# The maxima of full attention reach their rows by a transfer of two-byte elements, where a 32x32 transposition on VectorE stood

## The reference, cut to what matters

```
h = layernorm(x)
q, k, v = h @ Wq, h @ Wk, h @ Wv                 # 16 heads of 8
s = einsum('bhtd,bhsd->bhts', q, k) / sqrt(8)    # 1024 x 1024 for each batch and head
m = max(s, axis=-1)                              # one maximum for each query
e = exp(s - m)
out = (e @ v) / sum(e) @ Wo (+ bo)
x = x + out
```

## Time and profile before

| what | value |
|---|---|
| median of 3 runs | 1250.81 us (1248.14 to 1253.72) |
| the profiled execution's own time | 1252.19 us |
| its span in the profile | 1250.5 us |
| full attention, first layer, first to last splitting by POOL | 446.2 to 750.5 us |
| full attention, second layer | 874.2 to 1177.3 us |
| DVE busy over the whole span | 897.3 us, 72% |

### The profile page before, as it was taken

One profiled execution on the slowest core, in us unless ns is written; L12 is line 12 of the kernel. 1 busy time (PEld: TensorE's weight loads), 2 busy tenths in 40 slices (PEclk: granted clock), 3 DMA queues, 4 the chain that ended last, 5 costly groups with the idle time before them and its releaser, 6 DMA issues.

```text
span 1250.5 us, 32345 instructions
## 1 busy us (share of the span) xinstructions
PE 1065.1 (85%) x12934; PEld 532.7 (43%) x12934; DVE 897.3 (72%) x1221; ACT 741.3 (59%) x1496; POOL 184.7 (15%) x341
## 2 busy tenths in 40 slices
PE   6457887888648799999999998877999999999986
PEld 3135676764214333333334444533333344444443
DVE  4554554556465479999999991364899999999635
ACT  2250222223822339989999994222599899999921
POOL 9500434330008000000000000000000000000000
PEclk9668878779977799999999998678999999999977
DMA  2140212100000523322010100007322300101000
GB/s 82 64 126 23 85 56 85 52 2 1 1 0 0 174 83 67 70 48 49 18 29 18 26 21 20 0 1 227 59 62 52 77 20 20 26 20 27 19 14 34
DMA packets 65913, 58.05 MB, mean 46 GB/s; under 512 B 24944, under 2 KB 50032, under 8 KB 65648
## 3 DMA queue, kind: packets, MB, share of 16 engines
q1 hardware_dynamic: 65776, 56.14, 17.1%
HBM read 29.08 MB, written 26.84 MB: 45 GB/s over the span
## 4 chain that ended last, share of the span: by engine, by line
DVE 39%; PE 27%; issue 17%; POOL 8%; DMA 4%; ACT 3%; SPq 2%; POOLq 0%; DVEq 0%; ACTq 0%
DVE nmf L1355 33%; PE wide L565 16%; PE bank L565 10%; POOL big L535 4%; DMA KQs<-m_dram 3%; ACT xcsq L931 2%; DVE xcsq L1138 1%; DVE nmt L1364 1%; DVE res L1138 1%; SPq L371 1%; ACT big L931 1%; POOL KQs L502 1%; DVE big L1439 1%; DVE x L1138 1%; DMA kq_dram<-big 1%
## 5 line engine op out<-in xcount | busy, mean ns | idle before, releaser
L1355 DVE TENSOR_REDUCE nmf<-wide 128x1 f32<-128x1024 f32 x512 | 586.9, 1201 | 34.7 <-PE wide L565 34.5
L931 ACT ACTIVATE big<-wide 128x512 f32<-128x512 f32 (+2 forms) x773 | 441.9, 601 | 149.3 <-PE wide L565 116.1
L565 PE MATMUL bank<-big,V 128*9 128x128 f32 x8192 | 319.2, 274 | 11.8
L565 PE MATMUL wide<-big,KQs 48*128 48x512 bf16 x1024 | 308.0, 381 | 4.3 <-DVE nmf L1355 3.2
L931 ACT ACTIVATE big<-bank 128x512 f32<-128x512 f32 (+3 forms) x489 | 237.5, 506 | 82.4 <-PE bank L689 61.5
L565 PEld LDWEIGHTS bank<-big,V 128*9 128x9 f32 x8192 | 176.7, 90 | 232.2 <-ACT big L931 222.0
L565 PE MATMUL wide<-KQs,big 50*128 50x512 bf16 x683 | 233.5, 381 | 8.0 <-DMA KQs<-m_dram 6.9
L565 PE MATMUL bank<-KQs,big 50*128 50x512 bf16 x341 | 130.0, 381 | 4.2 <-DMA KQs<-m_dram 3.2
L547 POOL CAST nms<-nmf 128x4 bf16<-128x4 f32 x128 | 23.8, 186 | 715.5 <-DVE nmf L1355 715.5
L1302 DVE TENSOR_REDUCE nm<-wide 95x11 f32<-95x1408 f32 x32 | 51.7, 1620 | 57.5 <-PE wide L565 57.4
L565 PEld LDWEIGHTS wide<-KQs,big 50*128 50x128 bf16 x683 | 52.4, 93 | 83.4 <-ACT big L931 56.0
(11 more groups left out here) (190 smaller groups left out, 1050.6 us busy)
## 6 DMA issues: line engine op xcount, KB each, us to landing
kq_dram<-big SPq DMA_DIRECT2D x48, 256.0 KB, 4.1
o_dram<-big SPq DMA_DIRECT2D x128, 64.0 KB, 1.6
KQs<-k_dram SPq DMA_DIRECT2D x48, 132.0 KB
big<-kq_dram SPq DMA_DIRECT2D x32, 192.0 KB, 4.1
KQs<-kq_dram SPq DMA_DIRECT2D x32, 192.0 KB, 4.6
KQs<-q_dram SPq DMA_DIRECT2D x16, 293.9 KB
m_dram<-nmt SPq DMA_DIRECT2D x128, 8.0 KB
KQs<-m_dram SPq DMA_DIRECT2D x128, 2.0 KB
```

The source lines that it names most:

```text
L565: return nc.tensor.matmul(o, l, r, start=start, stop=stop, **kw)
L931: return nc.scalar.activation(o, i, f, **kw)
L1355: nc.vector.tensor_reduce(nmf[:, (s0 + i) % 4, c:c + 1], wide[:, k:k + 2, :].rearrange("p g c -> p (g c)"), AX.X, ALU.max, negate=True).th ...
```

## The change

DVE's transposition goes, with its semaphore nm_turned. SP now waits for POOL's split itself and sends columns 0 to 7 of nms straight to m_dram, with the two dimensions exchanged in the destination: the element of partition q and column j goes to row j, place q. Neighbours in the source are 256 bytes apart in the destination, so each two-byte element is a piece of its own. m_dram keeps its size; rows 8 to 31, which nobody read, are no longer written. `shift` is as before.

Two waits change with it. POOL may write a buffer of nms again only when the transfer that read it four slots earlier has landed (nm_out). DVE, before piece 0 of a slot, waits until POOL's split four slots earlier is done, because it reuses nmf; the transposition's wait used to cover that.

```
             def turned(i):
                 s = s0 + i
-                sp.wait_ge(nm_turned, s + 1)
-                sp.dma_start(m_dram[i, :, :].rearrange("j (g q) -> g j q", g=4),
-                             nmt[:, s % 4, :]).then_inc(nm_out[s % 4], 16)
+                sp.wait_ge(nm_split, s + 1)
+                sp.dma_start(m_dram[i, 0:8, :].rearrange("j q -> q j"),
+                             nms[:, s % 4, 0:8], allow_slow_non_contiguous=True).then_inc(nm_out[s % 4], 16)
...
         def split_shift(s):
             pool.wait_ge(mx_read, 4 * (s + 1))
             if s >= 4:
-                pool.wait_ge(nm_turned, s - 3)
+                pool.wait_ge(nm_out[s % 4], 16 * (s // 4))
...
             def maximum(i, c):
                 n = 4 * (s0 + i) + c
+                if c == 0 and s0 + i >= 4:
+                    dve.wait_ge(nm_split, s0 + i - 3)
                 dve.wait_ge(mx_ready, n + 1)
...
-            def turn(i):
-                s = s0 + i
-                dve.wait_ge(nm_split, s + 1)
-                if s >= 4:
-                    dve.wait_ge(nm_out[s % 4], 16 * (s // 4))
-                nc.vector.transpose(nmt[:, s % 4, :], nms[:, s % 4, :]).then_inc(nm_turned, 1)
-
             for i in range(SLOTS):
                 for c in range(4):
                     maximum(i, c)
-                    if c == 0 and i:
-                        turn(i - 1)
                 if i % H == 6 and i > H:
                     reciprocal(layer, i // H - 1)
-            turn(SLOTS - 1)
```

More of the change, by code:

```diff
@@ L195, in build @@
         mx_ready, mx_read = sem("mx_ready"), sem("mx_read")
-        nm_first, nm_split, nm_turned = sem("nm_first"), sem("nm_split"), sem("nm_turned")
+        nm_first, nm_split = sem("nm_first"), sem("nm_split")
         nm_out = [sem(f"nm_out{i}") for i in range(4)]
```

## The result

| | before | after |
|---|---|---|
| median of 4 runs of each, side by side | 1252.26 us | 2591.9 us (2582.0 to 2601.75) |
| ratio, 95% interval | | 2.071 [2.064, 2.079] |
| span of the profiled execution | 1250.5 us | 2599.7 us |
| POOL's first to last split, first layer | 304.3 us | 952.8 us |
| the same, second layer | 303.1 us | 954.9 us |

The forecast was 1302 us. The sign was right, the size was 26 times too small (1340 us more against 50), and the time lies far outside the range. The two attention layers hold 1300 of the 1349 us by which the span grew.

A forecast was written before the change was run, and what follows sets the result against it. DVE was taken to bound the ordinary slot at 4.62 us, the maxima's path almost as tight. With +34 us from 100 ordinary slots and +18 from 24 late ones, 1252.2 became 1304, as median 1302 us; range 1222 to 1410.

The forecast's parts named there:

- DVE sets the ordinary slot: Reductions and transposition on DVE set the slot's 4.62 us; without the transposition, 0.14 us less, 4.49.
- The path: Maxima's way from POOL's split through SP's transfers to PE's scores: a second bound, afterwards 3.50 us plus delay.
- slack of 2.0 us: From issue of the transfer back into qop to the scores, up to 2.0 us costs nothing.
- the saving of 0.72: Between POOL's end and SP's issue, the transposition's going takes 0.72 us a slot off the path.
- The DMA's pace of packets: In SP's queue, 1024 packets at 0.53 per ns take 1.98 us, making the transfer back 1.46 us later.
- rival A: Transfer out hides on 16 engines, 0.69 us for its packets, delay 0.17; kernel faster, 1225 us; chance 0.30.
- The transfer itself lands with a whole slot in hand: Transfer out to m_dram: its landing costs nothing, because `shift` of a slot is issued only a slot later.
- Rival C: Two-byte DRAM writes may cost more than 64-byte ones: 1399 us, or over 1800 at 24.6 ns; above 1400, chance 0.13.
- rate of 12 us for every 0.1 us a slot: Every 0.1 us that the transfer out's 1024 packets take beyond 1.6 us costs the kernel 12 us.
- B's better end: Rival that the change comes out even, 1258 us at worst; at a delay of 1.0, 1248 us; chance 0.09.
- The estimate from "VectorE: DVE Perf Modes": Transfer out's 1024 elements, by a page calling transposing plain DMA 19 times slower: 1.6 us, sum near no change.

The follow-up runs named there:

- e7: Kernel before without DVE's transposition, nms sent in the old 64-byte runs, exchange of partition and row left out: 1235.8 us beside 1251.7.
- e4: Kernel before plus one unread transfer a slot of 1024 two-byte elements into SBUF, each partition writing its own place: 1333.6 us beside 1254.0.
- e6: Kernel before without m_dram and transposition: eight transfers a slot write two-byte neighbours from nms straight into qop's rows in SBUF: 2047.7 us beside 1251.7.
- e1: Kernel before plus, in each slot, the changed kernel's transfer of 1024 two-byte elements to an unread DRAM tensor: 2622.3 us beside 1254.0.
- e5: Kernel before without m_dram and transposition: pieces take every fourth query, two transfers write eight-byte packets straight into qop's rows: 1239.6 us beside 1251.7.

## Why the prediction was wrong

*DVE sets the ordinary slot, and gains by the transposition's going: right, the size some 40% too large (0.13 for 0.09 us a slot).* e7 shows the reductions back to back and 4.53 us for the predicted 4.49.

*The path with its slack of 2.0 us and the saving of 0.72: right where it could be tried.* e4 gives 5.25 for a worked-out 5.23. In the changed kernel both terms are buried.

*The DMA's pace of packets: wrong, to the other side.* I took the common pace of 0.53 packets per ns of the earlier trace rows as a limit, 1.98 us for 1024. Behind an empty queue they pass in about 0.7 us, as rival A had it, 7.3 ns each on 16 engines. The nearness of two paces in rows of other shapes was a coincidence, and what the trace said of engine time per packet (10.8 ns) was the better guide. Quick packets delay the transfer back by 0.34 us (e4), not 1.46. Had this been all, the path would have given 3.50 + 0.34 = 3.84 and DVE's bound would have ruled: a gain of about 1%, as e7 shows it.

*"The transfer itself lands with a whole slot in hand": this is the step that failed.* I put all of the cost into the queue and gave the landing none beyond its packets. It takes 13 to 17 us, three slots' worth. All else follows from it: `shift` waits for it (944.9 us), transfers land one after the other, the next `shift` is held behind the next one, PE gets a slot's scores every 15.1 us, DVE starves, and PE's clock falls. 128 slots of 15.1 - 4.8 = 10.3 us are 1318 of the 1340 us, of which some 125 come from the slots beside the loads, when the DMA engines are busy with few bytes; that term wasn't in the prediction either.

*Rival C had the right sentence and the wrong mechanism and price.* A small write may cost more than the row of 64 bytes tells: true. But I priced it as time on an engine (up to 24.6 ns, a period of 9.3), and in the slots without loads the engines aren't busy (0.08 of the time), while the period is 14.0. Beside the loads, and in e6, they are, so the mechanism of C has a share there. Its rate of 12 us for every 0.1 us a slot was right (128 x 0.1 = 12.8); it was tied to the time of the packets, where it holds for the time to landing.

*B's better end* has a small slip: by the sum of the prediction a delay of 1.0 gives 1251 - 12 + 7 = 1246, not 1248.

The prediction quoted the Trainium skill, "DMA: Bandwidth & Descriptors", Specifications, that transfers under 512 bytes are read, modified and written. The runs bear it out only in part: neither 64 bytes nor two bytes alone in their piece (2.7 us) show a large price, but many small ones in one piece do. Such an update of a piece, one after another, is a reading that fits the table; no row shows the update itself. The estimate from "VectorE: DVE Perf Modes" (1.6 us, 19 times the transposing transfer) is short of the measured 14.6 by a factor of 9. From the first I should have made a rival that is priced by the landing, and given C more than 0.13.

What stays open: why 8 writes in 64 bytes cost 0.8 us and 16 cost 5 to 7, which size the piece has, and where between the last packet and the semaphore the time is spent. That a transfer behind lands late is shown for the one queue of SP, with 2 KB (e1) and with loads of 192 KB behind.

## What to carry over

When a transfer turns columns into rows, look at how many separate elements of it fall next to one another at the destination, not only at their number: the records of packets can look harmless while the landing takes over 10 us, and it then shows only in the time to landing and in who waits. Write neighbours in one piece of at least 8 bytes, here by letting a partition hold neighbouring queries (e5), or keep the transposition on an engine. And before a wait is called covered, price the time to landing by itself, since a slow landing also stops what is queued behind it.

## What the hardware showed that I had not expected

- 1024 elements of two bytes into DRAM land in 2.7 us at a step of 512 bytes and in 14.6 us at a step of two; into SBUF, 2.5 us when each partition writes its own place, while columns of 128 two-byte neighbours, eight transfers behind one another, have a median of 14.4.
- Behind an empty queue the engines are done with them within about 0.7 us (7.3 ns a packet), and the remaining time appears in no engine's busy share. With loads of 192 KB in the queue it does: 0.36 of the time busy at 18 GB/s, against 0.08 at 7 GB/s without them.
- A small transfer of another tensor, issued behind, took 12.5 and 13.6 us instead of some 1.6. In the changed kernel the packets of such a transfer had passed 3.6 us after its issue; it landed 14.7 us after it.
- Eight bytes an element are nearly free of it: 3.7 us in DRAM, 2.0 in SBUF; four bytes aren't (9.3).
- Loads of PE's weights from columns eight bytes apart took 118 ns for 94.
